# Node updates of the last two graph layers on TensorE's half arrays, with the vector pair products on GpSimd

## The reference

```python
u0 = einsum('nu,nv,uvw->nw', x0, a0, W_ss) + einsum('nuk,nvk,uvw->nw', x1, a1, W_vv)
u1 = einsum('nu,nvk,uvw->nwk', x0, a1, W_sv) + einsum('nuk,nv,uvw->nwk', x1, a0, W_vs)
x  = layernorm(x + x + merge(u0, u1) + linear(x0, x1))
```

## Time and profile before

| what | us |
|---|---|
| median of three runs | 21708.12 (21701.72 to 21713.34) |
| span of the profiled execution | 21748.2 |
| the first `nodes_update`, steady part of it | 16549.9 to 17928.0 of the span |
| TensorE busy in that part | 1319.02 of 1378.10 |
| VectorE busy in that part | 1160.39 |
| ScalarE, GpSimd busy in that part | 364.29, 54.57 |

### The profile page before, as it was taken

The page is one execution under the profiler, slowest core; times in us unless marked ns, Lnnn a source line. Parts: engine busy times, 40 slices in busy tenths (PEclk is TensorE's granted clock), DMA queues, the critical chain, the costliest instruction groups (busy, mean ns, idle before and its releaser), DMA issues. The chain is left out here.

```text
span 21748.2 us, 415044 instructions
## 1 busy us (share of the span) xinstructions
PE 17061.4 (78%) x99738; PEld 12888.6 (59%) x99738; DVE 17491.5 (80%) x45106; ACT 10278.5 (47%) x31430; POOL 12620.0 (58%) x13048
## 2 busy tenths in 40 slices
PE   2777666666579999999999999277778997777899
PEld 1333322222368888888888888155556885555688
DVE  3777788888768888888888989877777887777788
ACT  1222344444347777777777777033332223333222
POOL 2777666666447677666666766077772007777200
PEclk8888788888889999999999999599999999999999
DMA  2666555555664444444444444422222002222200
GB/s 87 171 171 171 144 112 111 111 111 112 140 200 123 123 122 123 121 121 122 123 122 122 123 122 121 124 60 60 61 61 27 6 10 64 61 61 61 28 6 6
DMA packets 1798610, 2131.88 MB, mean 98 GB/s; under 512 B 621200, under 2 KB 1473328, under 8 KB 1797904
## 3 DMA queue, kind: packets, MB, share of 16 engines
q0 software_dynamic: 567456, 1314.26, 22.9%
q1 hardware_dynamic: 1231088, 816.86, 15.5%
HBM read 1518.49 MB, written 611.44 MB: 98 GB/s over the span
## 5 line engine op out<-in xcount | busy, mean ns | idle before, releaser
L1624 PE MATMUL e_sums<-e_feat,e_same 128*128 128x272 f32 x13824 | 3449.5, 404 | 1348.7 <-ACT e_feat L1645 1291.9
L1606 POOL DMA_INDIRECT e_rows<-x,e_take x3456 | 3607.0, 1044 | 1127.1 <-issue 1045.8
L1624 PEld LDWEIGHTS e_sums<-e_feat,e_same 128*128 128x128 f32 x13824 | 2598.7, 193 | 2199.2 <-issue 1585.8
L629 PE MATMUL e_sums<-e_feat,e_same 128*128 128x480 f32 x3456 | 1961.6, 723 | 1317.3 <-DVE e_feat L697 1317.3
L613 POOL DMA_INDIRECT e_rows<-table,e_take x1728 | 1932.2, 1118 | 1307.0 <-issue 1280.0
L1200 ACT ACTIVATE e_m<-e_th,e_yt 128x64 f32<-128x64 f32 x6480 | 2300.9, 426 | 0.0
L629 PEld LDWEIGHTS e_sums<-e_feat,e_same 128*128 128x128 f32 x3456 | 800.0, 244 | 2478.8 <-issue 2388.7
L1062 POOL DMA_INDIRECT e_srow<-src_table,e_at x1620 | 1611.7, 995 | 927.1 <-issue 918.8
L1073 POOL DMA_INDIRECT comb<-e_crow,e_at x1620 | 1668.4, 1030 | 818.1 <-issue 510.8
L757 POOL TENSOR_TENSOR n_stats<-n_stats,n_power 128x1 f32<-128x1 f32 x250 | 145.1, 580 | 3411.3 <-DVE n_stats L742 3324.1
L648 ACT ACTIVATE e_feat<-e_feat,e_pay 128x64 f32<-128x64 f32 x5184 | 1284.8, 334 | 1755.3 <-DVE e_feat L672 1721.6
(11 more groups left out here) (322 smaller groups left out, 44182.6 us busy)
## 6 DMA issues: line engine op xcount, KB each, us to landing
e_pay<-pay_rows SPq DMA_DIRECT2D x432, 470.0 KB, 3.9
order_keys<-key_row SPq DMA_DIRECT2D x810, 128.0 KB
e_keys<-key_row SPq DMA_DIRECT2D x810, 128.0 KB
comb<-n_comb SPq DMA_DIRECT2D x600, 164.0 KB, 2.0
e_rows<-x,e_take POOLq DMA_INDIRECT x3456, 2.6
order_feat<-in_attr_T SPq DMA_DIRECT2D x810, 64.0 KB
e_basis<-in_attr_T SPq DMA_DIRECT2D x1620, 32.0 KB
e_comps<-in_attr_T SPq DMA_DIRECT2D x1620, 32.0 KB
```

What stands on the lines that cost most here:

```text
L629: ins = pe.matmul(sums[b][q // G][:, 0:AGG0], same[b][:, q, :], feat[b][:, q, 0:AGG0], start=q % G == 0, stop=q % G == G - 1)
L1606: pool.indirect_dma_start(out=rows[t.j][:, q, :], out_offset=None, in_=x, in_offset=bass.IndirectOffsetOnAxis(ap=take[t.j][:, q:q + 1], ax ...
L1624: ins = pe.matmul(sums[b][q // G][:, 512 * h:512 * h + HALF], same[b][:, q, :], feat[b][:, q, h * HALF:(h + 1) * HALF], start=q % G == 0, ...
```

## The change

- **Contraction.** `WQ` (64 columns) is now the stationary operand and `turnedT` moves (128 columns), so one matmul uses 64 of the array's 128 columns; the four chunks of a half alternate between the left and the right half of the array, which write partitions 0 to 63 and 64 to 127 of `ps_l[:, 256:384]`. What accumulates there is turned: features on partitions, nodes on columns, in two partial sums.
- **Fold.** ScalarE copies that tile to `foldT` in the step after (one copy of 128x128 ahead of the step's first `turnedT` copy); TensorE multiplies it by `twice`, two identities of 64 above each other, which adds both partial sums, turns them back and accumulates them on top of the linear part. The fold stands between turn 1 and contraction 0 of the next block, and `finish` waits for it (`folded`) where it waited for contraction 9.
- **Columns.** The weights `WZ` lie on all 128 partitions and the block's `a0T` on partitions 64 to 127, so that columns 0 and 2 use the upper row half of the array, 1 and 3 the lower.
- **Vector pairs.** GpSimd makes `vv` in three products of 128x1024, one for each component: two after its copy `own`, and the third after its power for block p. VectorE no longer makes `vv`.

```diff
                 def contract_half(b, h):
                     pe.wait_ge(half_sb, b.count(h + 1, HALVES))
                     for c in range(4):
-                        ins = pe.matmul(ps_l[b.j][:, 0:CS], turnedT[h % 2][:, c * P:(c + 1) * P], WQ[:, 4 * h + c, :],
-                                        start=False, stop=h == HALVES - 1 and c == 3)
+                        at = CS * (c % 2)
+                        ins = pe.matmul(ps_l[b.j][at:at + CS, FOLD:FOLD + P], WQ[:, 4 * h + c, :], turnedT[h % 2][:, c * P:(c + 1) * P],
+                                        start=False, stop=h == HALVES - 1 and c >= 2, skip_group_check=True)
                     ins.then_inc(half_used, 1)
+
+                def fold(p):
+                    pe.wait_ge(fold_sb, p.count(1))
+                    pe.matmul(ps_l[p.j][:, 0:CS], foldT[p.j][:, :], twice[:, :], start=False, stop=True, skip_group_check=True).then_inc(folded, 1)
...
-                    lhs = rowT[b.j][0:CS, 0:P] if n % 2 == 0 else a0T[b.j][:, :]
-                    pe.matmul(ps_z[n % 2][:, :], lhs, WZ[:, n * CH:(n + 1) * CH], start=True, stop=True).then_inc(z_ps, 1)
+                    lhs = rowT[b.j][0:CS, 0:P] if n % 2 == 0 else a0T[b.j][CS:P, :]
+                    at = CS * (n % 2)
+                    pe.matmul(ps_z[n % 2][:, :], lhs, WZ[at:at + CS, n // 2 * CH:(n // 2 + 1) * CH], start=True, stop=True).then_inc(z_ps, 1)
...
                             if h < HALVES - 1:
                                 turn_half(b, h + 1)
+                            if h == 0 and p.exists():
+                                fold(p)
                             contract_half(b, h)
...
             def _(act):
...
+                    if p.exists():
+                        act.wait_ge(half_used, p.count(HALVES, HALVES))
+                        act.activation(foldT[p.j][:, :], ps_l[p.j][:, FOLD:FOLD + P], ACT.Copy).then_inc(fold_sb, 1)
                     if b.exists():
                         for h in range(HALVES):
...
             def _(pool):
                 pool.wait_ge(blank, 1)
+
+                def vector_pairs(k, c):
+                    at = CS + CV * c
+                    return pool.tensor_tensor(vv[:, c * CV * CV:(c + 1) * CV * CV].rearrange("p (u v) -> p u v", u=CV),
+                                              bcast(row[k][:, at:at + CV].unsqueeze(2), (P, CV, CV)),
+                                              bcast(agg[k][:, at:at + CV].unsqueeze(1), (P, CV, CV)), ALU.mult)
...
-                    p = s.back(2)
+                    b, p = s.back(1), s.back(2)
+                    if b.exists():
+                        pool.wait_ge(row_in[b.j], b.dma())
+                        pool.wait_ge(agg_set, b.count(1))
+                        if b.reuses(1):
+                            pool.wait_ge(half_ps, b.count(0, HALVES))
+                        for c in two:
+                            vector_pairs(b.j, c)
                     if p.exists():
                         inverse_root(pool, stats[p.j][:, 8:9], power[:, 0:1], squares, roots, p, 1, 1)
+                    if b.exists():
+                        vector_pairs(b.j, 2).then_inc(vv_set, 1)
...
                 def pair_products(b):
...
-                    dve.tensor_tensor(vv[:, :].rearrange("p (c u v) -> p c u v", c=3, u=CV),
-                                      bcast(row[k][:, CS:D].rearrange("p (c u) -> p c u", c=3).unsqueeze(3), (P, 3, CV, CV)),
-                                      bcast(agg[k][:, CS:D].rearrange("p (c v) -> p c v", c=3).unsqueeze(2), (P, 3, CV, CV)),
-                                      ALU.mult).then_inc(vv_set, 1)
...
                 def finish(b):
                     k = b.j
                     links.start(b)
-                    dve.wait_ge(half_used, b.count(HALVES, HALVES))
+                    dve.wait_ge(folded, b.count(1))
```

More of the change, by code:

```diff
@@ L1712, in pair @@
             return [ph.sb(f"{name}{k}", shape) for k in two]
-        WZ, WQ, WL, WM = ph.sb("WZ", [CS, 4 * CH]), ph.sb("WQ", [P, 40, CS]), ph.sb("WL", [P, 2, D]), ph.sb("WM", [P, CHUNKS, D])
-        row, agg, a0T, rowT, accT, lastT = pair("row", [P, 2 * P]), pair("agg", [P, D]), pair("a0T", [CS, P]), pair("rowT", [P, 2 * P]), pair("accT", [P, 4 * P]), pair("lastT", [REST, P])
+        WZ, WQ, WL, WM = ph.sb("WZ", [P, 2 * CH]), ph.sb("WQ", [P, 40, CS]), ph.sb("WL", [P, 2, D]), ph.sb("WM", [P, CHUNKS, D])
+        row, agg, a0T, rowT, accT, lastT = pair("row", [P, 2 * P]), pair("agg", [P, D]), pair("a0T", [P, P]), pair("rowT", [P, 2 * P]), pair("accT", [P, 4 * P]), pair("lastT", [REST, P])
         own, ss = pair("own", [P, CAT]), pair("ss", [P, SQ])
         vv = ph.sb("vv", [P, 3 * CV * CV])
-        turnedT = pair("turnedT", [P, CH])
+        turnedT, foldT, twice = pair("turnedT", [P, CH]), pair("foldT", [P, P]), ph.sb("twice", [P, CS])
+        FOLD = 2 * P
         prod = ph.sb("prod", [P, 3 * 16 * 2 * CV])
@@ L1723, in nodes_update @@
         (wl, ready, scaled, blank, turned, turned_sb, agg_ps, agg_set, z_ps, z_used, reduced, ss_set, vv_set, half_ps, half_sb,
-         half_used, upd_set, squares, roots, new_set, linked, held) = (ph.sem(n) for n in (
+         half_used, fold_sb, folded, upd_set, squares, roots, new_set, linked, held) = (ph.sem(n) for n in (
              "weights", "ready", "scaled", "blank", "turned", "turned_sb", "agg_ps", "agg_set", "z_ps", "z_used", "reduced",
-             "ss_set", "vv_set", "half_ps", "half_sb", "half_used", "upd_set", "squares", "roots", "new_set", "linked",
+             "ss_set", "vv_set", "half_ps", "half_sb", "half_used", "fold_sb", "folded", "upd_set", "squares", "roots", "new_set", "linked",
              "held"))
@@ L1777, in messages @@
                     for c in range(CHUNKS):
-                        ins = pe.matmul(ps_a[0:CS, 2 * P:3 * P], WM[0:rows[c], c, 0:CS], lhs[c], start=c == 0, stop=c == CHUNKS - 1)
+                        ins = pe.matmul(ps_a[CS:P, 2 * P:3 * P], WM[0:rows[c], c, 0:CS], lhs[c], start=c == 0, stop=c == CHUNKS - 1)
                     ins.then_inc(agg_ps, 1)
@@ L1821, in step @@
                         for c in two:
-                            pe.matmul(ps_l[k][:, 0:D], rowT[k][:, c * P:(c + 1) * P], WL[:, c, :], start=c == 0, stop=False)
+                            pe.matmul(ps_l[k][:, 0:D], rowT[k][:, c * P:(c + 1) * P], WL[:, c, :], start=c == 0, stop=c == 1)
                         turn_half(b, 0)
@@ L1837, in step @@
                         messages(s)
-                run_steps(pe, step, 1, 2, NB)
+                    elif p.exists():
+                        fold(p)
+                run_steps(pe, step, 2, 2, NB)
             @block.scalar
@@ L1843, in _ @@
                 s_ss, s_vv, s_sv, s_vs, l_s, l_v = scales
-                halves = WZ[:, :].rearrange("p (w t z) -> p w t z", w=2, t=2)
-                act.mul(halves[:, :, 0, :], halves[:, :, 0, :], s_sv)
-                act.mul(halves[:, :, 1, :], halves[:, :, 1, :], s_vs)
+                act.mul(WZ[0:CS, :], WZ[0:CS, :], s_sv)
+                act.mul(WZ[CS:P, :], WZ[CS:P, :], s_vs)
                 act.mul(WQ[:, 0:32, :], WQ[:, 0:32, :], s_ss)
@@ L1866, in messages @@
                     act.activation(agg[k][:, :], ps_a[:, 0:D], ACT.Copy)
-                    act.activation(a0T[k][:, :], ps_a[0:CS, 2 * P:3 * P], ACT.Copy).then_inc(agg_set, 1)
+                    act.activation(a0T[k][CS:P, :], ps_a[CS:P, 2 * P:3 * P], ACT.Copy).then_inc(agg_set, 1)
                 def step(s):
-                    b = s.back(1)
+                    b, p = s.back(1), s.back(2)
+                    if p.exists():
+                        act.wait_ge(half_used, p.count(HALVES, HALVES))
+                        act.activation(foldT[p.j][:, :], ps_l[p.j][:, FOLD:FOLD + P], ACT.Copy).then_inc(fold_sb, 1)
                     if b.exists():
@@ L1884, in step @@
                             messages(s)
-                run_steps(act, step, 1, 2, NB)
+                run_steps(act, step, 2, 2, NB)
             @block.gpsimd
@@ L1903, in _ @@
                 dve.memset(power[:, :], -0.5)
+                dve.tensor_tensor(twice[:, :], g.ident[:, 0:CS], g.ident[:, CS:P], ALU.add)
                 for k in two:
@@ L2052, in update @@
     def update(name, ss, sv, vs, vv, lin_s, lin_v):
-        a[name + "_z"] = np.stack([sv.transpose(0, 2, 1).reshape(CS, 2, -1), vs.transpose(1, 2, 0).reshape(CS, 2, -1)], axis=2).reshape(CS, -1)
+        a[name + "_z"] = np.concatenate([sv.transpose(0, 2, 1).reshape(CS, -1), vs.transpose(1, 2, 0).reshape(CS, -1)])
         a[name + "_pairs"] = np.concatenate([ss.reshape(-1, CS), vv.reshape(-1, CS)])
```

4 lines of the change are left out of this document (1 added, 3 removed).

## The result

The changed kernel takes 21552.78 us (21546.76 to 21561.19, three runs) against 21708.12: 0.9938 of before, 95% interval 0.992 to 0.9956. That is 155 us less, clear of the 0.2% that a measurement can tell, and inside the range; the forecast itself was no change. The first update, from its first transpose of `row` to its last, went from 1355.2 to 1288.6 us and the second from 1354.2 to 1289.2, so 132 us of the gain lie in the two updates. The other 24 lie within the interval; the edge loops, which the change does not touch, differ by up to 27 us between the two profiles.

The account below looks back on a forecast made before the run. TensorE was taken to bound the kernel before, at 27.71 us a block. After the change, 26.6 with GpSimd holding VectorE plus 1.1 for clock falls made 27.7: no change, 21708 us, range 21400 to 21930.

Parts of the forecast that it names:

- the chain of waits: In each block GpSimd's products hold VectorE's q0, TensorE idles about 3.2 us for it, and the clock falls.
- Contraction: On TensorE: column halves work together, 0.46 us instead of 0.84, changes of shape cost nothing; a half takes 0.91.
- C: Rival: TensorE's column halves give nothing, a half takes 1.36 us; 114 us more, 21822; chance 0.20.
- GpSimd's product: Each vector-pair product of 128x1024 on GpSimd: taken as 2.4 us, lower bound 1.2.
- The holding: VectorE's q0 and normalisation wait until GpSimd's product is over; q0 runs from 25.4 to 26.5 us of a block.
- The period at full clock: One block before clock falls: 26.6 us, 1.1 below 27.71, set by GpSimd holding VectorE.
- The clock: TensorE's idle of about 3.2 us ahead of the first turn lowers its clock in two of three blocks: 1.13 us a block.
- A: Rival: TensorE's clock stays up, period 26.6 us; 106 us less, 21602; chance 0.20.
- B: Rival: GpSimd's product takes 1.2 us or doesn't hold VectorE, period 23.6; 394 us less, 21314; chance 0.13.
- D: Rival: TensorE's clock falls twice a block, period 30.0 us; 218 us more, 21926; chance 0.17.

Follow-up runs that it names:

- the two parts alone: Changed kernel with vector pairs back on VectorE: 0.9946 of before; kernel before with only the vector pairs moved to GpSimd: 0.9947 of before.
- e8_warm_half: Changed kernel plus 8 unread matmuls filling TensorE's wait for q0 ahead of a block's first turn: 0.9892 of the kernel before, period 25.40 us.
- e5_one_shape: Changed kernel with the turns too as matmuls on column halves, the contraction's shape: 0.9987 of the kernel before, period 27.31 us.
- e3_vv_two: Changed kernel with two buffers for the vector pairs, so GpSimd need not wait for the last turn: 0.9862 of the kernel before, period 24.14 us.
- e9_third_late: Changed kernel with GpSimd's third product waiting for the end of VectorE's normalisation: 0.9841 of the kernel before, period 24.38 us.
- e2_pairs_only: Kernel before with only the vector pairs moved to GpSimd, contraction and columns on the full array: 0.9947 of before, period 26.62 us.

## Why the prediction was right, and where it was off

The range held, but it is 530 us wide; the point forecast missed by 155 us, clear of noise. What came true is the chain of waits. The sizes in it were off both ways (the contraction came out dearer, GpSimd's products cheaper) and partly cancelled, which is luck.

**Contraction.** Right that the column halves work together: 0.44 without a change of shape. Wrong that the change of shape costs nothing; the row of one narrow transpose in the earlier trace rows did not carry that. It costs 0.15, on the way to the contraction and on the way back, so that a half takes 1.17 and not 0.91: by the half's time, C's 1.36 was nearer. The trace of the kernel before held the price, in the very L1778 that I took the contraction from: its eight instructions, whose shape differs from both neighbours, start at 17037.09, and the next group starts 1.02 later, where eight at 0.11 are 0.88:

```profile
17038.11 0.43 PE L1778 MATMUL n_ps_a<-n_lastT,n_WM 32*64 32x128 f32 x2
```

The Trainium skill's rule in "TensorEngine Tiling (Array Packing)", Key Properties, that a change of tiling mode drains TensorE, agrees with these runs, which put its price here at 0.15. The 0.26 a half moved contraction 6, the front and turn 8 back by 1.8 in seven halves; but turn 8 starts at 9.80 of a block instead of 9.14, since the sum had it wait for the third pair product. So about 0.7 of the 1.8 stayed on the path.

**GpSimd's product.** 1.91, two in a row 3.78: between the bounds of 1.2 and 2.4, and below the 2.4 I took. This is the term that was mis-sized most: two products ahead of q0 end after 3.78 and not 4.8, 1.0 off the period. The estimate of 2.25 from the Trainium skill's "GPSIMD Engine Reference", 3.1, would have been nearer (its 4497 ns is for an add with two inputs, not a product).

**The holding.** Right, in both places: q0 and the normalisation end just behind GpSimd's products. It is as the Trainium skill, "SBUF — State Buffer", section Who interferes with whom, has it: a product of two SBUF tiles on VectorE contends with GpSimd's reads. Wrong was that `own`'s copy would hold the normalisation too: that ended with the third product, and n0 started at 9.14 instead of 10.04, so that columns 3 started with columns 2 at 13.16 and did not wait for n1.

**The period at full clock** is 25.4 and not 26.6: about 1.0 of the difference is GpSimd's two products, the rest the columns that did not wait.

**The clock.** Right that it falls, and that falls make the long periods, as the 8 useless matmuls show. The reason I gave was weaker: I put TensorE's idle at 3.2, as long as the one in the earlier trace rows, and it is 1.8 to 1.95. That such waits suffice no row of before had shown. I took two falls in three blocks at 1.69; there are about three in four, each 1.3 to 1.6, and the mean over the short period is 1.06 where I had 1.13. That 1.06 and 1.13 are so near is luck as well.

So the forecast's chain was the kernel's, and its sum was 27.7 a block where 26.4 was measured. A gave 21602, nearer in number, but by the wrong cause: the clock does fall. B's cheap product without holding and D's two falls did not happen; C's halves that gain nothing did in part, a half gaining 0.11 of the 0.37 expected.

**The expected gain** of the two parts alone is 1.5 and 1.1 of the period, 2.6 together, and the change gained 1.27. With the falls gone (e8_warm_half) it gains 2.3, so most of what is missing is the clock. The added wait, two buffers and the pairs of halves brought back 4.1 in all.

## What to carry to other kernels

Moving work to an idle engine is not free when that engine shares a path with the one it relieves: look for what stands beside it in time, and put it beside instructions that it does not hold (here products from PSUM, 1.76, and reductions, 3.35, the same with and without GpSimd beside them). A wait of about 2 us on an otherwise full TensorE can cost more than its length (here 1.9, and 1.06 more on average for the clock), so such a wait ahead of a dense stretch is worth removing first. Matmuls of one shape should be grouped, and moving a hold is not removing it.

## What was not expected of the hardware

- Matmuls on two column halves run fully together (eight in 0.44, where eight at 0.11 one after the other would take 0.88), but each change between full and half columns costs 0.15 at full clock.
- A wait of 1.8 to 1.95 was followed in three blocks of four by TensorE at half its clock; in e5_one_shape the same wait was so in fewer than one of four. Waits of up to 0.9 (e3_vv_two, e9_third_late) never were.
- When GpSimd and VectorE both want SBUF, the one that waits goes next: GpSimd's two products in a row take 3.78 if VectorE comes after the second has begun, and 4.76 if it comes during the first (e2_pairs_only, e9_third_late).
- The normalisation, which reads one SBUF tile, is held as well (1.94 beside GpSimd's product, 0.36 without it); a product with one input from PSUM is not (1.76 in e9_third_late, beside GpSimd's third product, as in the kernel before).
